# First unit's row maxima over two key chunks as fp32 products of separately projected heads

## The chip, the cores and the metric

One core of one Trainium2 chip runs the whole program, one launch. The metric is the device time in microseconds. PE is the matrix engine, PEld its weight loads, DVE is VectorE, ACT ScalarE, POOL GpSimd, SP the engine that issues most DMAs.

## The reference

Two transformer layers over x of 2048 tokens x 128. Layer 0's attention has 16 heads of 8 columns over all 2048 keys; only that stands near the change.

```python
h = _layernorm(x, axis=-1) * (1 + ca) + sa
x = x + ga * _L0_attn_ref(h, ...)
# _L0_attn_ref:
q = (x @ Wq.T + bq).reshape(b, s, NHEADS, DK)      # NHEADS 16, DK 8, s 2048
k = (x @ Wk.T + bk).reshape(b, s, NHEADS, DK)
v = (x @ Wv.T + bv).reshape(b, s, NHEADS, DV)
w = jnp.einsum('bshd,bzhd->bhsz', q, k) / jnp.sqrt(jnp.float32(DV))
w = jax.nn.softmax(w, axis=-1)
vw = jnp.einsum('bhsz,bzhd->bshd', w, v).reshape(b, s, NHEADS * DV)
out = vw @ Wo.T + bo
```

Behind it stand layer 0's mixture of experts and layer 1 (a causal attention of 8 heads and a token mix).

## The kernel before, in words

Tokens go in four chunks of 512. A unit of layer 0 is one chunk of queries and one quad of four heads (16 units, `UNITS[0]`). For each unit the softmax's row maxima are taken first: 32 score tiles (four blocks of 128 queries, four key chunks, two pairs of heads), each two products of 128 queries x 512 keys into the two halves of a double bank S0 or S1 (`s`, L918), and one VectorE maximum over each (L1283). The maxima are turned into three bf16 rows (`neg`, `neg_turn`, L938, L1515) and sent by DMA into rows of Qs (L1942), so that the transposed scores (`st`, L958) come out shifted; ScalarE takes their exponential (L1530), and PE multiplies by the values (`pv`, L990). Maxima of the next unit run beside the exponentials of this one.

q and k of a head are stored as bf16 parts in 48 rows of Qs and Ks, so that one bf16 product over 48 rows has close to fp32 accuracy. To get there a chunk is projected in fp32 (`project`, L872), brought to SBUF by ScalarE with its bias (L1483, L1486), its high part is cast (L1490), the low parts are made by three steps (`split`, on VectorE L1222 to L1226 or on GpSimd L1684 to L1688), the three parts are stored to DRAM (L1897) and loaded again with heads placed on rows (`load`, L1911 for k, L770 for q). The splits of chunks use memory in turns (`split_memory`: three own places, then two of `qf` and `q3` alternately), so ScalarE waits with the next user of a place until the store of the last one has landed (`rows_stored`).

For chunk 0 and the first quad the path over DRAM is cut short: selection matrices (`pick`, in Vf) pick the parts of the heads by bf16 products into PSUM (L881, L889), and ScalarE (L1494) and VectorE (L1230) copy them to Ks and Qs.

`make_plan` writes one order of stages by hand and by due times; every engine walks it and takes its own part, in order. A PSUM bank (T0 to T2, O, S0, S1) is handed on in the order of `take`. Beside the 32 tiles of the first unit the plan puts the other projections, `mod`, `gates`, `rows` (small products with the modulation weights) and the four `values` (v of a chunk, L897), by the number i of the tile; i counts from 0 here, so tile 31 is the first unit's last.

## Time and profile before

| | us |
|---|---|
| median of 3 runs | 1084.54 |
| lowest, highest | 1083.62, 1086.57 |
| the profiled execution | 1081.58 |
| its span in the trace | 1079.9 |
| outside the span | 1.7 |
| PE, DVE, ACT, POOL busy | 1006.4, 900.6, 823.0, 195.7 |

Busy times of PE are modelled, with the latency of each product in it, so two products that overlap count as one stretch. All stretches below are in us from the start of the span. A row of the timeline merges instructions of one line that follow each other: start, length in all, engine, line, operation, output and inputs, the count of records, and in brackets how long the engine idled ahead and for whom. An fp32 product leaves two records, a bf16 one leaves one.

### The profile page before, as it was taken

Reading aid. Unit: us, or ns where it says so; the run is one execution under the profiler, and the core shown is the slowest. Engines: PE = TensorE matmul, PEld = TensorE weight load, DVE = VectorE, ACT = ScalarE, POOL = GpSimd, SP = SyncE. Lnnn points to the kernel's source line nnn. Section 1 sums busy time; section 2 is a strip of 40 time slices with the busy share of each in tenths; the row PEclk is TensorE's granted clock in tenths of the full one; section 3 lists DMA queues with packets and bytes.
Section 4 is the critical chain, followed back from the end, with each engine's and each line's share of the span. In section 5 each row is a group of like instructions: output and inputs, shape, how many; then the busy total and the mean of one; then the engine's idle time right before and its main releaser. Section 6 shows DMA issues by size and latency. Waiting matters only on the chain.

```text
span 1079.9 us, 22190 instructions
## 1 busy us (share of the span) xinstructions
PE 1006.4 (93%) x8662; PEld 341.5 (32%) x8662; DVE 900.6 (83%) x1153; ACT 823.0 (76%) x1580; POOL 195.7 (18%) x374
## 2 busy tenths in 40 slices
PE   6879999999999999999998899999989998899997
PEld 2322222222222222222232244333344563333324
DVE  8999999999999999999989677766778868897504
ACT  4249999998999998999987577576755676656785
POOL 4542200003000003000024200241042113110102
PEclk9679999999999999999999899999999999999997
DMA  3830511000000000000000441115200531200000
GB/s 99 182 102 9 140 32 28 4 2 2 2 2 2 2 2 2 2 2 2 3 2 30 149 131 45 40 34 93 35 2 9 147 100 40 32 10 1 1 11 11
DMA packets 46423, 41.68 MB, mean 39 GB/s; under 512 B 5599, under 2 KB 44479, under 8 KB 46319
## 3 DMA queue, kind: packets, MB, share of 16 engines
q1 hardware_dynamic: 44062, 34.87, 13.3%
q0 software_dynamic: 1824, 5.25, 1.7%
q8 instruction: 70, 1.15, 0.5%
q14 instruction: 35, 0.28, 0.1%
q10 hardware_dynamic: 432, 0.13, 0.0%
HBM read 26.44 MB, written 13.30 MB: 37 GB/s over the span
## 4 chain that ended last, share of the span: by engine, by line
PE 72%; DVE 13%; ACT 8%; issue 4%; DMA 1%; POOL 1%; SPq 0%; another core or an unknown queue 0%; ACTq 0%; DVEq 0%; POOLq 0%
PE O L990 26%; PE T L958 14%; DVE mx L1283 8%; PE S L918 8%; ACT PT L1530 5%; PE S L925 4%; PE T L967 4%; PE S L1105 2%; PE S L1071 1%; ACT PT L1524 1%; PE S L1061 1%; PE T L1113 1%; PE T L999 1%; PE S L967 1%; PE T L1093 1%
## 5 line engine op out<-in xcount | busy, mean ns | idle before, releaser
L1283 DVE TENSOR_REDUCE mx<-S 128x2 f32<-128x1024 f32 (+2 forms) x672 | 759.5, 1181 | 71.7 <-PE S L918 24.4
L1530 ACT ACTIVATE PT<-T 128x512 f32<-128x512 f32 (+2 forms) x1280 | 675.7, 580 | 116.8 <-PE T L967 49.1
L990 PE MATMUL O<-PT,Va 128*9 128x256 f32 (+1 forms) x4032 | 318.1, 387 | 3.3 <-ACT Os L1564 3.3
L918 PE MATMUL S<-Ks,Qs 48*128 48x512 bf16 x1024 | 204.4, 391 | 13.3 <-DVE mx L1283 11.2
L958 PE MATMUL T<-Qs,Ks 51*128 51x512 bf16 x1024 | 202.3, 387 | 12.1 <-ACT PT L1530 7.1
L958 PEld LDWEIGHTS T<-Qs,Ks 51*128 51x128 bf16 x1024 | 56.2, 93 | 223.8 <-issue 128.6
L990 PEld LDWEIGHTS O<-PT,Va 128*9 128x9 f32 x4032 | 59.8, 88 | 208.1 <-issue 198.5
L925 PE MATMUL S<-K,Qs 96*128 96x512 bf16 (+3 forms) x320 | 89.4, 349 | 5.0 <-DVE mx L1283 3.8
L967 PE MATMUL T<-Qs,K 99*128 99x512 bf16 (+3 forms) x256 | 67.4, 344 | 12.0 <-ACT PT L1530 8.3
L990 PE MATMUL O<-PT,V 128*17 128x512 f32 (+3 forms) x616 | 72.5, 540 | 0.0
L918 PEld LDWEIGHTS S<-Ks,Qs 48*128 48x128 bf16 x1024 | 52.5, 95 | 33.9 <-DVE mx L1283 27.5
L1796 POOL CAST n<-nm 128x16 bf16<-128x16 f32 x24 | 5.5, 228 | 307.3 <-DVE nm L1291 307.1
L1696 POOL TENSOR_SCALAR_AFFINE_SELECT PT<-PT 128x256 f32<-128x256 f32 x64 | 25.8, 408 | 132.8 <-ACT PT L1530 103.8
L925 PEld LDWEIGHTS S<-K,Qs 96*128 96x128 bf16 x320 | 28.3, 97 | 48.3 <-DVE mx L1283 18.9
L1811 POOL TENSOR_TENSOR vw<-om,rl 128x128 f32<-128x128 f32 x16 | 6.5, 407 | 183.7 <-DVE rl L1297 183.7
L967 PEld LDWEIGHTS T<-Qs,K 99*128 99x128 bf16 x256 | 19.3, 98 | 49.7 <-issue 36.9
L1524 ACT ACTIVATE PT<-S 128x1024 f32<-128x1024 f32 (+3 forms) x32 | 28.4, 943 | 2.7 <-PE S L967 2.5
L928 PE MATMUL S<-mq,idb 128*128 128x128 bf16 x128 | 25.7, 220 | 0.0
L1856 POOL DMA_INDIRECT XP<-sorted_y,posu x16 | 15.8, 990 | 38.7 <-DMA sorted_y<-Vf 34.5
L1515 ACT ACTIVATE nrow<-T 12x512 bf16<-12x512 bf16 x24 | 14.1, 586 | 11.4 <-PE T L938 11.0
L1246 DVE RECIPROCAL rl<-O 128x4 f32<-128x4 f32 x3 | 0.5, 172 | 26.3 <-PE O L1026 26.3
L1607 ACT ACTIVATE Vf<-S 128x512 f32<-128x512 f32 x16 | 9.5, 595 | 15.3 <-PE S L1061 11.4
(300 smaller groups left out, 825.6 us busy)
## 6 DMA issues: line engine op xcount, KB each, us to landing
Qs<-in_L_ffn_experts SPq DMA_DIRECT2D x28, 192.0 KB, 2.5
Ks<-in_L_ffn_experts SPq DMA_DIRECT2D x20, 192.0 KB, 2.5
Vf<-sorted_x SPq DMA_DIRECT2D x12, 256.0 KB, 4.5
sorted_y<-Vf SPq DMA_DIRECT2D x12, 256.0 KB, 2.3
Qs<-rows_q SPq DMA_DIRECT2D x24, 128.0 KB, 4.5
rows_q<-q SPq DMA_DIRECT2D x7, 384.0 KB, 2.5
Qs<-rows_q SPq DMA_DIRECT2D x36, 64.0 KB
sorted_x<-XP POOLq DMA_DIRECT2D x1, 1792.0 KB, 10.7
```

Source lines behind the costliest of these rows:

```text
L918: m = e.matmul(two[:, i, :], Qs[r0:r0 + 48, hp, q0:q0 + 128], Ks[r0:r0 + 48, hp, CH * kb:CH * kb + CH], start=True, stop=True, tile_positi ...
L925: m = e.matmul(two[:, i, 0:n], Q1[0:96, 4 * quad + 2 * pair + i, q0:q0 + 128], K1[0:96, CH * kb:CH * kb + n], start=True, stop=True)
L928: m = e.matmul(two[:, i, n - 128:n], idb[:, :], mq[:, :], start=False, stop=True, skip_group_check=True)
L958: m = e.matmul(bank, Ks[r0:r0 + 51, hp, keys], Qs[r0:r0 + 51, hp, CH * c:CH * c + CH], start=True, stop=True, tile_position=(r0, 0))
L967: m = e.matmul(bank[:, lo:CH], K1[0:99, keys], Q1[0:99, 4 * quad + 2 * pair + i, CH * c + lo:CH * c + CH], start=True, stop=True)
L990: m = e.matmul(acc[32 * g:32 * g + d1, lo:hi], v, PT[(2 * j + g // 2) % 4][:, p0 + lo:p0 + hi], start=fresh, stop=True, skip_group_check=n ...
L1105: m = e.matmul(two[:, h, 128 * k:128 * k + 128], w_of(g, 2 * p + k)[:, 128 * h:128 * h + 128], hS[p % 2][:, 128 * k:128 * k + 128], start= ...
L1283: e.tensor_reduce(mx[:, u % 2, h0:h0 + 2, kb], two[:, :, 0:n], AX.X, ALU.max).then_inc(free, 1)
L1524: e.activation(both, Sb[turn["st", L, j, 2 * pair][0]][:, :, lo:CH], ACT.Exp).then_inc(free, 1)
L1530: e.activation(PT[(2 * j + pair) % 4][:, CH * i + lo:CH * i + CH], bank[:, lo:CH], ACT.Exp).then_inc(free, 1)
L1696: e.affine_select(out=both, in_=both, compare_op=ALU.is_ge, fill=0.0, base=0, pattern=[[0, 2], [1, 128]], channel_multiplier=-1).then_inc( ...
L1856: e.indirect_dma_start(out=XP[:, t, :], out_offset=None, in_=sorted_y[g], in_offset=off(posu[:, t:t + 1])).then_inc(y_gathered[c], 16)
```

## The change

The picks are gone. For the first unit's tiles against key chunks 0 and 1 (`direct`: layer 0, unit 0, kb < 2, the first 16 tiles) the four heads are projected once more, in fp32, with weights whose columns are placed so that each of the four heads has its own 8 rows at 0, 32, 64 and 96 (`place_w`, two VectorE copies; `place_bias`, two products with a placed identity). ScalarE brings the results with bias to kd and qd in Vf. A score tile is then two fp32 products over 8 rows, in two row groups, in place of two bf16 products over 48 rows.

All row splits of layer 0 are now on GpSimd. Chunk 0 of q and k also goes over DRAM now, in another order: q0, k2, k3, k1, k0 and then q1 to q3 (`raw`, `load`). q0 and k2 are loaded in two parts (2 head pairs first, 6 later), the others whole. Chunk 3's norm moves from VectorE to ScalarE, with three more small GpSimd steps. wmod is loaded behind the first loads. `mod`, `gates`, `rows` and `values` stand closer together among tiles 17 to 30, and the halves of q1 to q3 at tiles 16 to 29.

```diff
 
-PARTS = {("k", c): 2 for c in range(4)} | {("q", 0): 2}
-
-PICKED = (("k", 0), ("q", 0))
-PART_OF = {"k": (0, 1, 2, 0, 1, 0), "q": (0, 0, 0, 1, 1, 2)}
+PARTS = {("q", 0): 2, ("k", 2): 2}
 
...
+
+
+def direct(L, u, qt, kb):
+
+    return (L, u) == (0, 0) and kb < 2
 
...
@@ -297,34 +292,38 @@
             setup1(s + 3, 3)
 
 
+    def raw(kind, c, bank):
+
+        P.project(kind, c, bank)
+        P.split(kind, c, "po")
+
+    def direct_rows(kind, i, bank):
+
+        P.take(("direct", kind, i), bank)
+        P.stage("direct", kind, i)
+
+    def load(kind, c, part=0):
+        P.stage("load", kind, c, part)
+
     P.stage("silu")
     P.stage("stats", 0, 0)
     P.take(("mod", 0), "T2")
     P.stage("mod", 0)
     P.norm(0, 0)
+    P.stage("place_w")
+    P.take(("place_bias",), "S0a")
+    P.stage("place_bias")
     P.turn_h(0, 0, "T0")
-    project("k", 0, "S1b")
+    direct_rows("q", 0, "T1")
     P.stage("bias_q")
     P.stage("stats", 0, 1)
-    project("q", 0, "S1a")
+    direct_rows("k", 0, "T2")
     P.stage("stats", 0, 2)
     P.norm(0, 1)
-    P.turn_h(0, 1, "T1")
+    direct_rows("q", 1, "O")
+    P.turn_h(0, 1, "T0")
     P.stage("stats", 0, 3)
     P.norm(0, 2)
-    split("k", 0, "dv")
-    split("q", 0, "dv")
-    load_slabs()
-    for kind, pair, bank in (("k", 0, "S0a"), ("q", 0, "S0b"), ("k", 1, "S1b"), ("q", 1, "S1a")):
-        P.take(("pick", kind, pair), bank)
-    P.norm(0, 3)
-    P.stage("pick_high")
-    project("k", 1, "T2")
-    split("k", 1, "po")
-    for kind, pair in (("k", 0), ("q", 0), ("k", 1), ("q", 1)):
-        P.stage("pick", kind, pair)
-    P.turn_h(0, 2, "T0")
-    load_slabs()
 
     def values(c):
         P.take(("v", c), ("O", "T2")[c % 2])
...
@@ -474,35 +473,43 @@
 
     for i in range(many[0]):
         emit_s()
-        if i == 1:
-            project("k", 2, "O")
-            split("k", 2, "po")
-            P.stage("wmod_loads")
-            P.turn_h(0, 3, "T1")
-            load_slabs()
+        if i == 0:
+            raw("q", 0, "T1")
+        elif i == 1:
+            P.turn_h(0, 2, "T0")
+            P.norm(0, 3)
         elif i == 3:
-            project("k", 3, "T2")
-            split("k", 3, "po")
-            load_rest(("k", 0))
-            load_slabs()
-            load_rest(("k", 1))
+            raw("k", 2, "T2")
+            load("q", 0)
+        elif i == 4:
+            P.turn_h(0, 3, "T0")
+        elif i == 5:
+            direct_rows("k", 1, "T1")
+            load("k", 2)
+        elif i == 7:
             P.stage("broadcast")
-        elif i in (5, 7, 9, 11, 13, 15):
-            project_q(1 + (i - 5) // 4, (i - 5) // 2 % 2)
-            if i == 7:
-                load_rest(("q", 0))
-            elif i == 11:
-                load_rest(("k", 2), ("k", 3))
-            elif i == 15:
+            raw("k", 3, "O")
+        elif i == 10:
+            raw("k", 1, "T2")
+            load("q", 0, 1)
+            load("k", 3)
+        elif i == 13:
+            raw("k", 0, "T1")
+            load("k", 2, 1)
+            load("k", 1)
+            load("k", 0)
+        elif i in (16, 18, 23, 25, 27, 29):
+            project_q(*((1, 0), (1, 1), (2, 0), (2, 1), (3, 0), (3, 1))[(16, 18, 23, 25, 27, 29).index(i)])
+            if i == 18:
                 P.stage("constants")
-        elif i == 18:
+        elif i == 17:
             beside("mod", 1)
+        elif i == 19:
+            beside("gates")
         elif i == 20:
-            beside("gates")
-        elif i == 22:
             beside("rows")
-        elif i in (25, 27, 29, 31):
-            values((i - 25) // 2)
+        elif i in (21, 22, 26, 30):
+            values((21, 22, 26, 30).index(i))
     for i in range(7):
         if i == 2:
             urgent.pop(0)[1]()
...
-        pick = Vf[:, 0:768].bitcast(BF16).rearrange("p (k s h m) -> p k s h m", k=2, s=3, h=2)
+        kd, qd = Vf[:, 0:1024].rearrange("p (c n) -> p c n", c=2), Vf[:, 1024:1536]
+        placed_w = {"k": Vf[:, 1536:1664], "q": Vf[:, 1664:1792]}
+        idp, bd = Vf[:, 1792:1920], Vf[:, 1920:1922]
         hS, tS, acS = ([Vf[:, 6656 + 512 * k + 256 * i:6656 + 512 * k + 256 * i + 256] for i in range(2)] for k in range(3))
         Kf = Ks[:, :, :].rearrange("p a n -> p (a n)")
...
                         m.then_inc(full, 1)
-                elif name == "pick_high":
-                    pe.wait_ge(picks_made, 12)
-                    for k, kind in enumerate(("k", "q")):
-                        pe.wait_ge(high_part, P.slot[kind, 0] + 1)
-                        for pair in range(2):
-                            bank, _ = opened(("pick", kind, pair))
-                            e.matmul(bank, pick[:, k, 0, pair, :], split_memory(kind, 0)[3][:, 0, :], start=True, stop=False)
-                elif name == "pick":
-
-                    kind, pair = a
-                    bank, full = opened(("pick", kind, pair))
-                    k = int(kind == "q")
-                    pe.wait_ge(low_parts["dv"], P.split_eng[kind, 0][1])
-                    for part in (1, 2):
-                        m = e.matmul(bank, pick[:, k, part, pair, :], split_memory(kind, 0)[3][:, part, :], start=False, stop=part == 2)
-                    m.then_inc(full, 1)
+                elif name == "place_bias":
+                    bank, full = opened(("place_bias",))
+                    pe.wait_ge(ld_w0, 64)
+                    pe.wait_ge(id_placed, 1)
+                    e.matmul(bank[:, 0:1], idp, bk[:, :], start=True, stop=True)
+                    e.matmul(bank[:, 1:2], idp, bq[:, :], start=True, stop=True).then_inc(full, 1)
+                elif name == "direct":
+                    kind, i = a
+                    bank, full = opened(("direct", kind, i))
+                    c, n0, n1 = (i, 0, CH) if kind == "k" else (0, 256 * i, 256 * i + 256)
+                    done(("turn", 0, c))
+                    pe.wait_ge(w_placed, 2)
+                    e.matmul(bank[:, n0:n1], placed_w[kind], hc(c, n0, n1), start=True, stop=True).then_inc(full, 1)
                 elif name == "values":
                     (c,) = a
                     bank, full = opened(("v", c))
...
                     q0 = CH * c + 128 * qt
-                    if L == 0:
+                    if direct(L, u, qt, kb):
+                        done(("direct", "k", kb))
+                        done(("direct", "q", qt // 2))
+                        for i in range(2):
+                            r0 = 32 * (2 * pair + i)
+                            m = e.matmul(two[:, i, :], qd[r0:r0 + 8, q0:q0 + 128], kd[r0:r0 + 8, kb, :], start=True, stop=True,
+                                         tile_position=(r0, 0))
+                    elif L == 0:
                         rows_in(c, quad, pair, kb)
                         hp = 2 * quad + pair
                         for i in range(2):
...
                     m.then_inc(free, 1)
+                elif name == "place_w":
+                    dv.wait_ge(ld_w0, 64)
+                    e.tensor_copy(from_32(placed_w["k"]), by_head(wkT[:, :])).then_inc(w_placed, 1)
+                    e.tensor_copy(from_32(placed_w["q"]), by_head(wqT[:, :])).then_inc(w_placed, 1)
+                elif name == "place_bias":
+                    bank, free = filled(("place_bias",))
+                    e.tensor_copy(bd[:, 0:1], bank[:, 0:1])
+                    e.tensor_scalar(bd[:, 1:2], bank[:, 1:2], 8.0 ** -0.5, None, ALU.mult).then_inc(free, 1)
                 elif name == "bias_q":
                     dv.wait_ge(ld_w0, 64)
                     e.tensor_scalar(bqs[:, :], bq[:, :], 8.0 ** -0.5, None, ALU.mult).then_inc(bq_scaled, 1)
...
                     e.activation(parts[:, 0, :], f, ACT.Copy).then_inc(high_part, 1)
-                elif name == "pick" and a[0] == "k":
-                    kind, pair = a
-                    bank, free = filled(("pick", kind, pair))
-                    e.activation(Ks[0:112, pair, 0:CH], bank[0:112, :], ACT.Copy).then_inc(free, 1)
+                elif name == "direct":
+                    kind, i = a
+                    bank, free = filled(("direct", kind, i))
+                    done(("place_bias",))
+                    if kind == "k":
+                        e.activation(kd[:, i, :], bank, ACT.Identity, bias=bd[:, 0:1], scale=1.0).then_inc(free, 1)
+                    else:
+                        half = slice(256 * i, 256 * i + 256)
+                        e.activation(qd[:, half], bank[:, half], ACT.Identity, bias=bd[:, 1:2], scale=8.0 ** -0.5).then_inc(free, 1)
+                elif name == "norm" and a == [0, 3]:
+                    ac.wait_ge(ln_normed[0], 3)
+                    ac.wait_ge(ln_scale[0], 4)
+                    passed(P.xh_prev[0, 3])
+                    for t in range(12, 16):
+                        m = e.activation(x_hat(0, t), xs[:, t, :], ACT.Identity, bias=nb[:, t - 12:t - 11], scale=rs[:, t:t + 1])
+                    m.then_inc(ln_normed[0], 1)
                 elif name == "values":
                     (c,) = a
...
             e.dma_start(bv[:, :], col(A["L0_attn_bv"])).then_inc(ld_v, 16)
+            e.dma_start(wm_sb[0][:, 256:768], A["L0_wmod"][:, 256:768]).then_inc(ld_wm, 16)
+            e.dma_start(wm_sb[1][:, 0:768], A["L1_wmod"]).then_inc(ld_wm, 16)
             for name, *a in order:
                 if name == "split":
                     kind, c = a
```

How the order of instructions moves, at the three places of which the prediction speaks. First PE from the first projections on. L872 projects, L859 turns a chunk, L881 and L889 are the picks, L918 the score tiles. Before:

```order
L872 MATMUL S<-hT,wkT 128x512
L872 MATMUL S<-hT,wqT 128x512
L859 MATMUL T<-idf,xh 128x128 x4
L881 MATMUL S<-PT,Vf 128x512 x4
L872 MATMUL T<-hT,wkT 128x512
L889 MATMUL S<-PT,Vf 128x512 x8
L859 MATMUL T<-idf,xh 128x128 x4
L918 MATMUL S<-Ks,Qs 128x512 x4
```

The same place in the changed kernel, where L894 are the placed projections, L866 the turn, L922 the fp32 tiles and L879 a projection for the row parts:

```order
L894 MATMUL T<-hT,Vf 128x256
L894 MATMUL T<-hT,Vf 128x512
L894 MATMUL O<-hT,Vf 128x256
L866 MATMUL T<-idf,xh 128x128 x4
L922 MATMUL S<-Vf 128x512 x2
L879 MATMUL T<-hT,wqT 128x512
L922 MATMUL S<-Vf 128x512 x2
L866 MATMUL T<-idf,xh 128x128 x4
L922 MATMUL S<-Vf 128x512 x4
L879 MATMUL T<-hT,wkT 128x512
L922 MATMUL S<-Vf 128x512 x2
```

The picks between projection and tiles are gone, and whole 512-column products now stand among the tiles.

Second, SP's queue around the store of q1 (`rows_q<-q3`, the first of them), with what each waits for. Before:

```order
L1911 DMA Ks<-rows_k 8x6x512
L1897 DMA rows_q<-q3 128x3x512 [waits low_parts_po]
L770 DMA Qs<-rows_q 8x6x512 [waits rows_stored1]
L770 DMA Qs<-rows_q 8x6x512 x11
L1897 DMA rows_q<-q3 128x3x512 [waits low_parts_po]
L1911 DMA Ks<-rows_k 24x6x512
L1911 DMA Ks<-rows_k 16x6x512
```

Changed kernel, from the load of k0 on:

```order
L1952 DMA Ks<-rows_k 24x8x512 [waits rows_stored3]
L1952 DMA Ks<-rows_k 16x8x512
L1952 DMA Ks<-rows_k 8x8x512
L1952 DMA Ks<-rows_k 24x8x512
L1952 DMA Ks<-rows_k 16x8x512
L1952 DMA Ks<-rows_k 8x8x512
L1938 DMA rows_q<-q3 128x3x512 [waits low_parts_po]
L1969 DMA Ks<-K1 3x8x2048 [waits po_const]
L1969 DMA Ks<-K1 3x8x2048
L1938 DMA rows_q<-q3 128x3x512 [waits low_parts_po] x2
L1978 DMA Qs<-nrow 3x512 [waits free_T0]
```

The store of q1 stood ahead of the second parts of q0, k2 and k3; now it stands behind every load of k.

Third, PE at the end of the first unit; L897 or L901 are `values`, here of chunk 3 into T2. Before, tiles 30 and 31, `values`, and the next unit's first tile:

```order
L918 MATMUL S0<-Ks,Qs 128x512 [waits free_S0]
L918 MATMUL S0<-Ks,Qs 128x512
L918 MATMUL S1<-Ks,Qs 128x512 [waits free_S1]
L918 MATMUL S1<-Ks,Qs 128x512
L897 MATMUL T2<-wvT,hT 128x128 [waits free_T2]
L897 MATMUL T2<-wvT,hT 128x128 x3
L918 MATMUL S0<-Ks,Qs 128x512 [waits q_loaded0_1,k_loaded0_1,free_S0]
```

Changed kernel, from the second half of q3 (L879) on:

```order
L879 MATMUL T2<-hT,wqT 128x256
L929 MATMUL S0<-Ks,Qs 128x512 [waits free_S0]
L929 MATMUL S0<-Ks,Qs 128x512
L901 MATMUL T2<-wvT,hT 128x128 [waits free_T2]
L901 MATMUL T2<-wvT,hT 128x128 x3
L929 MATMUL S1<-Ks,Qs 128x512 [waits free_S1]
L929 MATMUL S1<-Ks,Qs 128x512
L929 MATMUL S0<-Ks,Qs 128x512 [waits q_loaded0_1,k_loaded0_0,free_S0]
```

and ScalarE beside it (L1503 brings a chunk of q to `qf`, L1510 casts it, L1530 copies `values` to Va):

```order
L1503 ACTIVATE qf<-T1,bqs 128x512 [waits rows_stored3,full_T1]
L1510 ACTIVATE q3<-qf 128x512 [waits free_T1]
L1530 ACTIVATE Va<-O 128x64x8 [waits full_O]
L1503 ACTIVATE qf<-T2,bqs 128x512 [waits rows_stored4,full_T2]
L1510 ACTIVATE q3<-qf 128x512 [waits free_T2]
L1530 ACTIVATE Va<-T2 128x64x8 [waits full_T2]
```

q3 now uses T2 directly ahead of `values` of chunk 3, and tile 31 stands behind both.

## Rows read from the trace of the kernel before

**Rows 1.** The page, part 2: busy tenths of VectorE in 40 slices.
```profile
DVE  8999999999999999999989677766778868897504
```
**Rows 2.** Windows of 40 us: busy (instructions) per engine, PEclk, DMA share, GB/s.
```profile
core 0: us, PE busy (x) PEld busy (x) DVE busy (x) ACT busy (x) POOL busy (x), PEclk, DMA share, GB/s
120.00:160.00 40.00, 39.42 (x420) 9.08 (x416) 39.50 (x37) 38.17 (x72) 4.14 (x32) 1.00 0.38 96
```
**Rows 3.** Timeline of VectorE's maxima: start, us, engine, line, operation, count.
```profile
20.84 4.79 DVE L1283 TENSOR_REDUCE mx<-S 128x2 f32<-128x1024 f32 x4
...
26.14 17.53 DVE L1283 TENSOR_REDUCE mx<-S 128x2 f32<-128x1024 f32 x15 [0.50 <-PE S L918]
...
59.59 1.22 DVE L1283 TENSOR_REDUCE mx<-S 128x2 f32<-128x1024 f32 x1
...
60.98 12.80 DVE L1283 TENSOR_REDUCE mx<-S 128x2 f32<-128x1024 f32 x11
```
**Rows 4.** Timeline of PE: projections, a turn and the first score tiles.
```profile
10.93 2.08 PE L872 MATMUL S<-hT,wkT 128*128 128x512 f32 x2 [0.87 <-ACT hT L1474]
...
12.80 1.92 PE L872 MATMUL S<-hT,wqT 128*128 128x512 f32 x2
...
16.92 1.10 PE L872 MATMUL T<-hT,wkT 128*128 128x512 f32 x2 [0.15 <-ACT hT L1474]
...
19.88 0.60 PE L859 MATMUL T<-idf,xh 128*128 128x128 f32 x4
...
20.41 0.81 PE L918 MATMUL S<-Ks,Qs 48*128 48x512 bf16 x4
```
**Rows 5.** Timeline of PE: score tiles, `mod`, `values`, a half of `pv`.
```profile
28.55 0.39 PE L918 MATMUL S<-Ks,Qs 48*128 48x512 bf16 x2 [0.74 <-DVE mx L1283]
...
30.82 0.61 PE L918 MATMUL S<-Ks,Qs 48*128 48x512 bf16 x2 [0.56 <-DVE mx L1283]
...
42.00 2.72 PE L832 MATMUL T<-cs,XP 128*128 128x1 f32 x12
...
56.66 1.16 PE L897 MATMUL O<-wvT,hT 128*128 128x128 f32 x8
...
79.37 0.62 PE L990 MATMUL O<-PT,Va 128*9 128x256 f32 x8
```
**Rows 6.** Timeline of ScalarE and GpSimd: cast and first split steps of a chunk.
```profile
23.23 0.63 ACT L1490 ACTIVATE q<-qf 128x512 bf16<-128x512 f32 x1
...
23.94 1.15 POOL L1684 TENSOR_TENSOR qf<-qf,q 128x512 f32<-128x512 f32 x1 [1.39 <-ACT q L1490]
...
25.16 0.61 POOL L1686 CAST q<-qf 128x512 bf16<-128x512 f32 x1
```
**Rows 7.** Timeline of SP's queue: stores (L1897) and loads (L1911) of row parts.
```profile
32.41 0.39 SPq L1897 DMA_DIRECT2D rows_k<-q  x1
32.84 7.13 SPq L1911 DMA_DIRECT2D Ks<-rows_k  x18
40.02 0.39 SPq L1897 DMA_DIRECT2D rows_q<-q  x1
...
53.61 0.38 SPq L1897 DMA_DIRECT2D rows_q<-q  x1
```
**Rows 8.** Issues of q1's and q3's store (last number: us to landing); ScalarE's wait.
```profile
rows_q<-q SPq DMA_DIRECT2D x1, 384.0 KB, 6.7
...
rows_q<-q SPq DMA_DIRECT2D x1, 384.0 KB, 7.8
...
46.79 0.69 ACT L1483 ACTIVATE qf<-T,bqs 128x512 f32<-128x512 f32 x1 [9.87 <-DMA rows_q<-q]
```
**Rows 9.** Windows of 10 us, columns as in rows 2.
```profile
30.00:40.00 10.00, 9.24 (x26) 2.83 (x24) 9.73 (x9) 2.63 (x4) 7.80 (x10) 0.50 0.85 195
40.00:50.00 10.00, 9.28 (x40) 5.99 (x38) 8.21 (x12) 1.96 (x4) 1.77 (x3) 0.50 0.87 173
50.00:60.00 10.00, 7.54 (x50) 4.64 (x48) 10.00 (x10) 2.08 (x5) 1.43 (x3) 0.99 0.74 173
```
**Rows 10.** Timeline of PE: the first transposed scores.
```profile
67.86 0.61 PE L958 MATMUL T<-Qs,Ks 51*128 51x512 bf16 x2 [0.47 <-DMA Qs<-nrow]
```

49 lines of the change are left out of this document (21 added, 28 removed).

## The prediction

> **What bounds the kernel now.** I read the page first. VectorE is at 9 tenths in the first half of the span [rows 1], and the windows of 40 us give it 39.50 us of work in 40 there [rows 2]: for the sixteen units of layer 0 its row maxima set the pace, PE merely looks as full (its ends are modelled). So what counts is when this stream of maxima starts and whether it is ever broken before it is steady. The timeline of VectorE shows both [rows 3]: the first maximum starts at 20.84, 15 of them in one piece take 17.53 (1.17 us each), the last of the first unit starts at 59.59, and the next unit's 11 follow without a gap. The whole first unit (32 maxima, 37.4 us at 1.17) takes 38.75 us from its first start to its last start, where 31 x 1.17 = 36.3 would do: 2.5 us are lost, mostly to the cold `mod` job of 2.72 us [rows 5]. Any shift of the maximum of tile 31 goes through to the end one for one, since a stretch 39.50/40 full can't take it back.
>
> **Part 1, the start.** Removed ahead of the first maximum: VectorE's six split steps and its two pick copies, twelve pick products. The two whole projections run from 10.93 to 14.72 [rows 4]; the change streams the same 1024 columns (256 + 512 + 256) through the placed weights, so it is at 14.7 too. Then stands the turn of chunk 1 (0.60 at the full clock [rows 4], up to twice that at half), so the first fp32 tile may start at 15.6. ScalarE's evictions of kd and qd (0.69 at 512 columns [rows 8]) lie beside the later products. VectorE's small new copies (some 0.5 us) lie ahead of 15.6.
>
> **Part 2, the price of an fp32 tile.** The trace has none with two row groups. Upper bound: two products one behind the other, 2 x 1.10 less an overlap of ends, 1.95. Lower bound: one product alone, 1.10 the project of 16.92 [rows 4]. I take 1.08, near the lower one, because both row groups ran side by side in bf16 (two records, 0.39 together) and four column groups of fp32 ran side by side (eight records, 0.62) [rows 5]. Where the granted clock is 0.50 (1.2 GHz) the bf16 tile takes 0.61 instead of 0.39 [rows 5, 9]. The projects at 10.93 and 12.80 took 2.08 and 1.92, that at 16.92 took 1.10 [rows 4]: by their durations the first two ran at the half clock and the last at 2.4 GHz. PE has no hole from 10.9 on in the new order either, so I take the full clock for the tiles; at half a tile would take 1.95.
>
> Now the walk through the 16 fp32 tiles. Among them stand six 512-column products (q0, k2, k3, k1, k0, direct k1) and two turns: 16 x 1.08 + 6 x 1.10 + 2 x 0.60 = 25.1. Ends overlap the next start by 0.17 within one kind (7 times; 0.21 at half clock, where the project at 12.80 starts before the end of the one at 10.93 [rows 4]) and by 0.08 at a change of kind (16 times; the tile at 20.41 starts 0.07 before the turn's end at 20.48 [rows 4]): -2.5. S0 and S1 come free 1.22 after a maximum starts [rows 3], which makes PE wait 1.1 in all. So PE ends tile 15 at 15.6 + 23.7 = 39.3; VectorE began at 16.7, was short of a tile after each job (3.5 us in sum), and starts tile 16 at 40.8. Before it starts it at 26.14 + 12 x 1.17 = 40.2. The four microseconds won at the start are gone by tile 16: part 2 is worth about +0.6 us. Tiles 16 to 31 are bf16 again at 0.39, with thirteen jobs among them; at 2.4 GHz the same walk has VectorE at tile 31 at 59.0, 0.6 before the old 59.59. That alone would be no change.
>
> Here a page speaks against the change: the Trainium skill, "TensorEngine Tiling (Array Packing)", Key Properties, says that a change of tiling mode drains the array. The row at 20.41 shows a smaller overlap, not a full drain. With a full drain the 16 changes would give up 16 x 0.08 = 1.3 us more, which would move the no-change case below by +1.3.
>
> **Part 3, the chain behind the row transfers.** This is the term that decides. The old kernel took unit 0's chunk 0 from PSUM by the picks and loaded the rest early. The new one must send q0 and k2 through memory first, and the loads of k1 and k0, whole, come last (the order of SP). The order shows a new chain: ScalarE's eviction of q3 waits for `rows_stored4`, that is for the store of q1; SP issues this store behind the loads of k2, k1 and k0; PE's `values` of chunk 3, ahead of tile 31, wants T2, which is free only when q3 is evicted; and PE is in order, so tiles 31 and up wait. So does unit 1's first tile, for k0 itself.
>
> When does it start? POOL's split takes 1.15 + 0.61 + 1.15 and ScalarE's two steps 0.69 + 0.63 [rows 6, 8]. In my walk k1's product ends at 33.0, ScalarE at 34.4, POOL at 37.4: SP stores k1 at 37.4. Up to and with the store of q1 follow 8 transfers: stores of k1, k0, q1 (3 x 384 KB), q0 for 6 heads (576), k3 (768), k2 for 6 heads (576), k1 and k0 (2 x 768) = 4608 KB. SP's own issuing (0.38 each) is done by about 53.5, also with the wait for k0's store, which comes out of 6.7 us of queue like q1's store before [rows 7, 8]. How long the bytes take: the trace moved 173 GB/s from 40 to 60 [rows 9], which gives 27.3 us; the old kernel's own queue had from the store at 32.41 to the landing of q3's store at 53.61 + 7.8 = 61.4 [rows 7, 8] exactly the same 4608 KB (4 stores, 4 k loads of 576, one of 192, q0's 576), 29 us. So landing between 64.7 and 66.4; since these stretches weren't always fed, I take 65.
>
> Then: eviction 0.69, `values` at 1.2 GHz after an idle PE (1.16 at the full clock [rows 5], so some 2.0), tile 31 0.61 [rows 5]: VectorE starts tile 31 at 65 + 0.69 + 2.0 + 0.61 = 68.3, against 59.59: **+8.7 us**. The shift rows follow by the same chain (old first transposed score at 67.86 [rows 10], new about 76.5), so nothing else becomes late. The old kernel had the same form of wait, hidden: ScalarE stood 9.87 us for q1's store until 46.79 [rows 8], with no `values` behind it.
>
> The Trainium skill, "DMA: Bandwidth & Descriptors", on how many engines a DMA uses, says that a copy with 8 rows runs on 8 of the 16 engines. By that the fullest engine carries 384 KB here against 376 KB in the old 29 us, and the landing would be at 67.0; no row here shows single engines.
>
> **Sum.** -4.1 at the start, +4.7 by the fp32 tiles and their jobs, -1.2 by the second half, then a wait of 9.3 for the transfers: +8.7. The norm of chunk 3 on ScalarE, wmod's earlier load (behind x in the queue) and POOL's extra steps cost nothing: ScalarE has little to do there (2.63 us of work from 30 to 40 [rows 9]), and POOL would be through with k0's split some 3 us before SP comes to its store. On the profiled execution 1081.58 + 8.7 = 1090.3; it lies 3.0 under the median of the three runs, so against the median: 1084.54 + 8.7 = 1093.2.
>
> **Rivals.** (A) The forecast, slower by the transfer chain: landing of q1's store between 61 and 68 moves tile 31 by 4.7 to 11.7, 1089.2 to 1096.2. It decides as soon as the store lands after 55.9, when `values` 3 could start; 4608 KB from 38.4 on would need 270 GB/s for that, and no window of ten microseconds has over 195 [rows 9]. Chance 0.60. (B) The transfers are nearly in time: whole-chunk loads make fewer, bigger transfers, and a share of 0.74 to 0.87 of the DMA engines [rows 9] leaves some room. Then the walk holds, -0.6 to +3: 1084 to 1087.5, a little less if ends overlap more. Chance 0.20. (C) PE paces: row groups don't overlap in fp32, or the eight-row products leave the clock at 1.2 GHz. With 1.95 a tile the walk ends at 72.2 instead of 59.6, and with the queue behind it +12 to +16, 1096 to 1100; with the low level all through up to +27, 1111. For it: no such row exists. Against it stands the side by side of [rows 5]. Chance 0.12. (D) Faster: the jobs slip between the tiles without stopping VectorE, transfers in time. Then up to 4.1 of the start and up to 2 of the old stalls are won, 1078.5 to 1081. Chance 0.08.
>
> **Numbers.** A measurement of this kernel can tell about 0.3%, 3.3 us. Faster: D and a bit of B, 0.09. Slower: A, C, and none of B, of A all but the lowest tenth: 0.68. Same: 0.23. The range 1083 to 1100 leaves out D, the lower edge of B (together 0.13) and the far part of C (0.07).
>
> **What would show it.** In the new trace: first maximum at about 16.7 (18 or more means PE still at 1.2 GHz); fp32 tiles of 1.1 (rows of 1.9: C); tile 16 near 41; ScalarE's last eviction of q waiting for "DMA rows_q" until about 65, a gap of 8 to 10 us in VectorE's maxima ahead of tile 31 or 32; the first transposed scores at about 76; the windows from 120 on unchanged. I am wrong if that gap is missing or ends before 60, or if layer 0 takes the shift back.

## The result, and the profile after

The changed kernel takes 1111.25 us (median of 4 runs, 1106.61 to 1112.79) beside 1085.55 us for the kernel before on the same chip (4 runs, 1083.62 to 1086.61): a ratio of 1.0237, 95% interval 1.0218 to 1.0256, **25.7 us slower**. The forecast was 1093.2 us with a range of 1083 to 1100. Its sign was right, its size was not, and the range did not hold the time. The span of the profiled execution is 1109.4 us.

VectorE's row maxima again show the whole story (timeline of VectorE after; columns: start, us, engine, line, operation, tiles, count, then in brackets the idle time before it and who ended it). To be held against [rows 3].

```profile
16.73 1.23 DVE L1303 TENSOR_REDUCE mx<-S 128x2 f32<-128x1024 f32 x1 [1.42 <-PE S L922]
...
33.33 2.36 DVE L1303 TENSOR_REDUCE mx<-S 128x2 f32<-128x1024 f32 x2 [2.79 <-PE S L922]
...
52.19 4.85 DVE L1303 TENSOR_REDUCE mx<-S 128x2 f32<-128x1024 f32 x4 [2.79 <-PE S L922]
...
68.67 9.15 DVE L1303 TENSOR_REDUCE mx<-S 128x2 f32<-128x1024 f32 x8 [0.18 <-PE S L929]
84.97 1.23 DVE L1303 TENSOR_REDUCE mx<-S 128x2 f32<-128x1024 f32 x1 [7.15 <-PE S L929]
```

The first maximum starts at 16.73 (16.7 forecast). The group at 52.19 is tiles 14 to 17, so tile 16 starts at 54.6 where 40.8 was forecast. Tile 31 starts at 84.97, behind a wait of 7.15. In the kernel before it was 59.59 [rows 3], so tile 31 is 25.4 us late: -4.1 at the start, +18.5 over the first sixteen tiles (37.9 us from the first maximum to tile 16 instead of 19.4), +3.9 over tiles 16 to 30, +7.15 by the wait. These four come to 25.4, and the whole kernel is 25.7 us longer.

Where the 18.5 us come from stands in the windows (us of the window, busy us and instructions of each engine, PEclk, DMA share, GB/s), which answer to [rows 9]:

```profile
core 0: us, PE busy (x) PEld busy (x) DVE busy (x) ACT busy (x) POOL busy (x), PEclk, DMA share, GB/s
15.00:20.00 5.00, 5.00 (x19) 2.07 (x19) 2.69 (x4) 2.72 (x5) 1.99 (x4) 0.90 0.00 2
20.00:25.00 5.00, 5.00 (x12) 1.56 (x12) 2.43 (x3) 2.70 (x7) 2.13 (x3) 0.50 0.23 79
25.00:30.00 5.00, 5.00 (x13) 1.72 (x10) 1.91 (x2) 1.38 (x2) 4.18 (x6) 0.50 0.06 22
...
60.00:65.00 5.00, 5.00 (x20) 3.21 (x20) 2.75 (x4) 2.37 (x5) 3.15 (x4) 0.50 0.89 174
65.00:70.00 5.00, 4.62 (x26) 3.20 (x26) 3.71 (x4) 1.20 (x2) 0.00 (x0) 0.82 0.88 128
```

TensorE is busy 5.00 us of 5 from 15 to 30, and still its granted clock falls from 1.00 (2.4 GHz) to 0.50 (1.2 GHz) just before 20 us (0.90 in that window) and stays there to about 67 (0.82 in the last window). The rows of TensorE (timeline; 8*128 8x512 are the operands' shapes) show what that does:

```profile
15.54 1.14 PE L922 MATMUL S<-Vf 8*128 8x512 f32 x4
16.61 1.12 PE L879 MATMUL T<-hT,wqT 128*128 128x512 f32 x2
17.67 1.13 PE L922 MATMUL S<-Vf 8*128 8x512 f32 x4
...
22.13 2.08 PE L879 MATMUL T<-hT,wkT 128*128 128x512 f32 x2
24.14 2.08 PE L922 MATMUL S<-Vf 8*128 8x512 f32 x4
```

At the full clock an fp32 tile takes 1.14 (1.08 forecast): its two row groups do run side by side. At half it takes 2.08 (1.95 forecast), and so do the projections among the tiles. VectorE needs 1.2 us a tile and stands idle for the rest.

The transfers (timeline of SP's queue, which answers to [rows 7]; L1938 stores, L1952 loads) and then ScalarE's timeline with its wait, as in [rows 8]:

```profile
47.27 0.38 SPq L1938 DMA_DIRECT2D rows_k<-q  x1
...
55.11 14.78 SPq L1952 DMA_DIRECT2D Ks<-rows_k  x18
69.93 0.67 SPq L1938 DMA_DIRECT2D rows_q<-q  x1
70.64 3.76 SPq L1969 DMA_DIRECT2D Ks<-K  x2
```

```profile
81.57 0.69 ACT L1503 ACTIVATE qf<-T,bqs 128x512 f32<-128x512 f32 x1 [8.37 <-DMA rows_q<-q]
```

q1's store is issued behind 18 loads of 2112 KB in all, which take 14.78 us to issue (before: 18 of 1344 KB in 7.13 [rows 7]), and lands at 81.5. ScalarE waits 8.37 us for it with q3's eviction, and the wait of 7.15 ahead of tile 31 follows. That is the forecast's chain, every link of it.

### The profile page after: what moved, and what is told of

Read it like the earlier page. It is cut to its first block, busy times and chain, and to the rows that moved or that the text cites. A ratio compares the mean times of both kernels' runs of the same rounds, so it can differ in the third digit from the quotient of the medians.

```text
span 1109.4 us, 22247 instructions
## 1 busy us (share of the span) xinstructions
PE 1029.5 (93%) x8694; PEld 351.1 (32%) x8694; DVE 895.2 (81%) x1134; ACT 827.9 (75%) x1586; POOL 202.6 (18%) x382
## 3 DMA queue, kind: packets, MB, share of 16 engines
q1 hardware_dynamic: 44398, 35.27, 13.2%
## 4 chain that ended last, share of the span: by engine, by line
PE 70%; DVE 10%; ACT 8%; DMA 4%; issue 4%; SPq 2%; POOL 1%; another core or an unknown queue 1%; ACTq 0%; DVEq 0%; POOLq 0%
PE O L1001 25%; PE T L969 14%; PE S L929 8%; DVE mx L1303 6%; ACT PT L1562 4%; PE S L936 4%; PE T L978 3%; PE S L1116 2%; PE S L922 2%; DMA rows_q<-q 1%; PE S L1082 1%; ACT PT L1556 1%; PE T L879 1%; PE S L1072 1%; PE T L1124 1%
## 5 line engine op out<-in xcount | busy, mean ns | idle before, releaser
L929 PE MATMUL S<-Ks,Qs 48*128 48x512 bf16 x992 | 197.2, 388 | 10.4 <-DVE mx L1303 8.1
L929 PEld LDWEIGHTS S<-Ks,Qs 48*128 48x128 bf16 x992 | 50.8, 95 | 29.0 <-DVE mx L1303 21.9
L922 PE MATMUL S<-Vf 8*128 8x512 f32 x64 | 22.1, 1075 | 2.1 <-DVE mx L1303 2.1
L1362 DVE SCALAR_TENSOR_TENSOR Vf<-Vf,S 128x512 f32<-128x512 f32 x16 | 10.9, 682 | 14.9 <-ACT Vf L1639 14.0
```

Of the source, the lines that this page charges most:

```text
L922: m = e.matmul(two[:, i, :], qd[r0:r0 + 8, q0:q0 + 128], kd[r0:r0 + 8, kb, :], start=True, stop=True, tile_position=(r0, 0))
L929: m = e.matmul(two[:, i, :], Qs[r0:r0 + 48, hp, q0:q0 + 128], Ks[r0:r0 + 48, hp, CH * kb:CH * kb + CH], start=True, stop=True, tile_positi ...
```

## The experiments

The kernel before ran on the same chip each time; the last column is the difference of the medians to it, and the intervals are those of the ratio, at 95%. "First st" is the first transposed score (67.86 before [rows 10]), which sums up what the first unit lost: in the timed kernels it shifts by 4 to 25 us, and the time follows it within 3.4 us. All edits are shown shortened. e4, e7 and e16 add up the scores of several heads in the first 16 tiles, so they show times and not a usable kernel.

| kernel | tile 16 starts | wait ahead of tile 31 or 32 | first st | us against before |
|---|---|---|---|---|
| before | 40.2 | none | 67.86 | 0 |
| after | 54.6 | 7.15 | 93.06 | +25.7 |
| after again (e15) | 52.6 | 8.96 | 90.92 | +23.75 |
| q3 moved (e10) | 57.4 | none | 91.57 | +21.2 |
| q3's own place (e3) | 52.5 | 3.25 | 87.18 | +19.0 |
| 32 rows (e1) | 43.6 | 8.36 | 83.17 | +13.75 |
| 64 rows (e7) | 41.1 | 9.75 | 82.88 | +14.3 |
| 64 rows, k0 first, q3 moved (e16) | 42.6 | none | 78.96 | +7.9 |
| bf16 (e2) | 35.4 | 9.33 | 76.76 | +7.85 |
| bf16, q3's own place (e5) | 36.7 | 4.90 | 74.22 | +5.0 |
| the same, k0 first (e6) | 34.9 | 1.48 | 72.11 | +3.3 |

**The clock, and the width of the products.** Four kernels change the tiles alone (columns of the windows below as above). In e1, e7 and e4 the products go over more rows of the array:

```
-  qd[r0:r0 + 8, q0:q0 + 128], kd[r0:r0 + 8, kb, :]      tile_position=(r0, 0), r0 = 32 * (2 * pair + i)
+  qd[r0:r0 + 32, ...], kd[r0:r0 + 32, ...]              e1: the further 24 rows are zero
+  qd[r0:r0 + 64, ...], kd[r0:r0 + 64, ...]              e7: r0 = 64 * i, two heads added up
+  qd[:, ...], kd[:, ...]                                e4: no tile_position, all heads added up
```

> The changed kernel with one edit: the fp32 tiles take all 32 rows of each row group instead of the 8 of the head; the 24 others hold zeros, so the result is the same. Theory 1: PE's clock falls at 20 us because the fp32 tiles use only 16 of 128 rows at a time, so that the chip counts PE as little used. If rows by instruction count (not by value), the granted clock stays at 1.00 from 20 to 50, the tile stays at 1.14, tile 16 starts near 41 instead of 54.6, and the time falls by 7 to 14 us to about 1097 to 1104 (the store of q1 then still holds tile 31 up, near 68 to 75). Rival 2: the clock falls for another reason (the waits between tiles, or just the time since the start): windows 20 to 50 at 0.50, tiles 2.08, 1111 as the changed kernel. Rival 3: it is the values that count (zeros are no work): as rival 2.

> The changed kernel with each fp32 tile's two products over 64 rows each (rows 0 to 63 beside rows 64 to 127, still two row groups side by side), so that all 128 rows take part; a product then adds up two heads, so the scores of those 16 tiles are not the reference's, their size and order are. Theory 1 (the clock falls because few rows of the array take part; with the pair still side by side): granted clock 1.00 through 20 to 55 us, tile 1.14, tile 16 at 41 to 43, tile 31 behind the wait for q1's store at 68 to 72, time before + 8 to + 12 us: what is left is the transfer chain alone. Rival (the fall comes from two fp32 products running side by side, and the 128-row version that kept the clock did so because its products ran one behind the other): clock down to 0.50 from about 20 as in the changed kernel, tiles 2.08, before + 24 to + 27.

> The changed kernel, but each of the two fp32 products of the first 16 tiles runs over all 128 rows, one behind the other, without row groups. Leaves out the separation of heads in these 16 tiles (the scores of four heads are summed), so their maxima are others. Shows the clock and the price of a tile without row groups: theory 1 has the granted clock at 1.00 throughout 20 to 50, as all rows are in use; a tile takes 1.95 to 2.1 (twice 1.10 less overlap) at the full clock, tile 16 starts near 52. If the clock still falls to 0.50, a tile takes 3.9 and the time is near 1135 to 1140, and theory 1 is out.

Measured: e1 1090.7 us (+13.75, ratio 1.0131, 1.0103 to 1.0158), e7 1092.19 (+14.3, 1.0141, 1.0111 to 1.0170), e4 one run, 1098.83 (+21.9). The windows of e1, e7 and e4, in this order, and of e16 (the table's other kernel with 64 rows):

```profile
25.00:30.00 5.00, 5.00 (x20) 1.50 (x18) 4.01 (x4) 2.00 (x3) 3.53 (x6) 1.00 0.33 98
30.00:35.00 5.00, 4.80 (x16) 1.19 (x14) 2.79 (x3) 1.32 (x2) 2.53 (x4) 0.67 0.23 59
...
45.00:50.00 5.00, 5.00 (x20) 3.46 (x20) 3.03 (x7) 0.84 (x2) 0.00 (x0) 0.50 0.97 156
```

```profile
25.00:30.00 5.00, 5.00 (x20) 1.67 (x18) 3.49 (x4) 2.00 (x3) 3.01 (x6) 1.00 0.34 99
...
45.00:50.00 5.00, 5.00 (x34) 3.31 (x32) 4.93 (x5) 2.58 (x6) 3.15 (x4) 1.00 0.98 163
```

```profile
30.00:35.00 5.00, 5.00 (x13) 2.28 (x12) 2.63 (x3) 1.36 (x3) 1.33 (x3) 1.00 0.39 117
...
45.00:50.00 5.00, 5.00 (x14) 2.04 (x13) 2.90 (x3) 1.32 (x2) 2.31 (x3) 1.00 0.61 145
```

```profile
40.00:45.00 5.00, 4.42 (x27) 2.33 (x23) 4.75 (x6) 0.53 (x1) 2.91 (x3) 0.96 0.67 152
45.00:50.00 5.00, 5.00 (x18) 3.25 (x18) 3.37 (x6) 1.91 (x3) 2.31 (x3) 0.50 0.99 147
```

With 8 rows a group the clock falls just before 20 us (in e15 at 22 to 23). With 32 it holds past 31 us, comes back for three us before 40 and is then low to 55. With 64 beside 64 it holds through all sixteen fp32 tiles: to 50 in e7, to about 44.6 in e16. With 128 it holds past 50. From 15 to 30 us, where the first kernels part, they have the same columns, the same place in the program and a TensorE that is busy 5.00 of 5. So the busy time does not tell them apart, and the rows that the products take part in do. e7 also answers the rival that the pair side by side in fp32 is the cause: the pair is kept there, every one of its tiles takes 1.13, and the clock stays. e1's further rows hold only zeros, so what they gain does not come from their values. Each width has one trace, 64 rows two and 8 rows four, and why rows should count is not shown. e4 also shows what a tile costs without the pair: 1.88 us.

VectorE's timeline of e7:

```profile
38.77 4.62 DVE L1303 TENSOR_REDUCE mx<-S 128x2 f32<-128x1024 f32 x4 [0.89 <-PE S L922]
...
55.19 3.49 DVE L1303 TENSOR_REDUCE mx<-S 128x2 f32<-128x1024 f32 x3 [4.45 <-PE S L929]
...
74.80 1.23 DVE L1303 TENSOR_REDUCE mx<-S 128x2 f32<-128x1024 f32 x1 [9.75 <-PE S L929]
```

The first group is tiles 14 to 17: with the clock up, tile 16 starts at 41.1 against the 40.8 of the forecast. From the first maximum (16.16) that is 24.9 us, where the changed kernel took 37.9 and the kernel before 19.4. So 13.0 of the 18.5 us are the clock's, and 5.5 (4.7 forecast) are the price of the fp32 tiles and their jobs at the full clock. In the time of the whole kernel the clock is worth less, 9.5 us against e15 and 11.4 against the first measurement, since earlier tiles then wait longer for the transfers (4.45 and 9.75 above).

Of the expectations, e1's time came (7 to 14 us less than the changed kernel), its clock of 1.00 to 50 us did not. e7's clock to 50, its tiles and tile 16 came; its tile 31 (68 to 72) and its time (+8 to +12) did not. e4's clock came, its tile 16 starts at 50.7 (52).

e2 puts the direct rows into bf16 (a tile is 0.39 then):

```
-  kd, qd = Vf[:, 0:1024]..., Vf[:, 1024:1536]
+  kd, qd = Vf[:, 0:512].bitcast(BF16)..., Vf[:, 1024:1280].bitcast(BF16)
```

> The changed kernel with kd and qd as bf16 instead of fp32, so that a tile is two bf16 products over 8 rows in two row groups (one pass, 512 columns). The maxima are then less exact, which the softmax only sees as another shift. Takes away the fp32 price alone. If the fp32 tiles at half clock (2.08) are what paces the first 16 tiles, each tile now takes 0.39 or 0.61 and what is left are the six whole projections (2.08 at half clock): tile 16 near 40 to 43 instead of 54.6, tile 31 then held by the store of q1 until 68 to 75; time 1095 to 1103. If other things pace them (ScalarE, the order of jobs), the time stays within 4 us of 1111. The clock: theory 1 (few rows) has it at 0.50 here as well.

Measured: 1084.8 us, +7.85 (1.0067, 1.0046 to 1.0087). Tile 16 starts at 35.4 (40 to 43 expected), five us ahead of the kernel before, and the clock, expected at 0.50 here too, holds to about 29 us. The five us are lost again, as VectorE's timeline of e2 shows:

```profile
50.20 9.14 DVE L1303 TENSOR_REDUCE mx<-S 128x2 f32<-128x1024 f32 x8 [0.70 <-PE S L929]
68.68 1.23 DVE L1303 TENSOR_REDUCE mx<-S 128x2 f32<-128x1024 f32 x1 [9.33 <-PE S L929]
```

The transfer chain alone puts tile 31 at 68.68, though these tiles hardly hold VectorE up.

**The chain.** e3 gives q3's rows a place (and a semaphore) of their own, so that their eviction waits for no store. e10 leaves the places and moves q3's two half projections from beside tiles 27 and 29 to behind tiles 35 and 37.

```
 def split_memory(kind, c):
+    if n == 7:
+        return 5, 0, Vf[0:rows, 2048:2560], Vf[0:rows, 2560:3328]...        e3
...
-        elif i in (16, 18, 23, 25, 27, 29):
+        elif i in (16, 18, 23, 25):                                          e10
...
+        if i in (3, 5):
+            project_q(3, i // 4)
```

> The changed kernel with one wait taken away by memory: chunk 3 of q gets its own place for fp32 and bf16 parts, so ScalarE's eviction of q3 no longer waits for the store of q1 (8.37 us in the trace of the changed kernel, ahead of a 7.15 us gap in VectorE's maxima before tile 31). Theory A (this chain costs the gap): the gap shrinks to 0 to 2 us and the time falls by 5 to 7.5, to 1104 to 1106. Rival: the load of k0, which the next unit's first tile wants, lands no earlier than the store of q1 did, so the gap moves behind tile 31: the time falls by under 3 us, and the new gap is ahead of tile 32 and waits for DMA Ks<-rows_k.

> The changed kernel with one move alone: q3's projections, its eviction and its three low parts come after tiles 35 and 37, behind the row of negative maxima, instead of beside tiles 27 and 29. Products, types and places are the changed kernel's. Theory (the gap of 7.15 us ahead of tile 31 is q3's eviction waiting for q1's store and nothing else, and the start of the transposed scores carries it to the end): no such gap, tile 31 at 77 to 78 in a trace like the changed kernel's, first transposed scores at 85 to 88 instead of 93, and 18 to 20 us above the kernel before instead of 25.7. Rival (the stores and loads as a whole are late, so the gap only moves to tile 32 or to the transposed scores): a gap of the same length there, 24 to 26 above before.

> The changed kernel itself once more, beside the others. Theory (8 rows in fp32 bring the granted clock down as soon as these tiles fill TensorE): 24 to 28 us above the kernel before; tiles 2.08 us from between 15 and 21 us to 55 at least, tile 31 at 84 to 87, first transposed scores at 92 to 95. Rival (the fall at 20 us was the luck of one execution): the low stretch begins 5 us later or more, or ends earlier, and the time is under before + 20.

Measured: e3 1095.93 us, +19.0 (1.0185, 1.0145 to 1.0224); e10 1098.32, +21.2 (1.0186, 1.0167 to 1.0204); the changed kernel itself once more (e15) 1101.47, +23.75 (1.0232, 1.0205 to 1.0259), its clock falling at 22 to 23 us, three later than in the first trace; the time is just under the 24 to 28 expected. In both repairs the long wait ahead of tile 31 is gone (VectorE of e10, where these nine are tiles 23 to 31):

```profile
72.42 10.27 DVE L1305 TENSOR_REDUCE mx<-S 128x2 f32<-128x1024 f32 x9 [0.89 <-PE S L931]
```

So q3's eviction behind q1's store is what held tile 31. But beside e15 e3 wins 4.8 us and e10 2.5, less than e15's wait of 8.96 (and the intervals of e3 and e15 overlap): in e3 tile 32 then has a wait of 3.25 us, for k0's rows by what e6 below shows (the trace names no releaser), so theory and rival both came in part. e10 missed its 18 to 20. And e10's execution ran its tiles at the low clock from the first on:

```profile
15.51 2.08 PE L924 MATMUL S<-Vf 8*128 8x512 f32 x4
17.52 2.08 PE L881 MATMUL T<-hT,wqT 128*128 128x512 f32 x2
```

```profile
20.00:25.00 5.00, 5.00 (x17) 1.66 (x15) 1.52 (x2) 3.26 (x7) 2.92 (x3) 1.00 0.00 0
```

The second fence is the window of that same trace: it says 1.00 beside products that take 2.08. The row is wrong there; durations decide. The Trainium skill, "TensorE: Matmul & The Clock Gate", Part 1, warns that the recorded clock events can be unreliable, and this trace agrees: 2.08 us under a 1.00.

This bears on the comparison of 8-row kernels. The longest executions of the changed kernel (1112.79), of e15 (1102.95, 1105.40), e3 (1102.25) and e10 (1099.03, 1099.25) have a recorded mean clock of 0.979 to 0.985, the shorter ones 0.956 to 0.968. By e10's trace the higher record can mean a low stretch that was not recorded; for the others no trace shows it. Among executions with the lower record e15 takes 1098.27 and 1099.99, e10 1096.48 and 1097.61, e3 1094.19 to 1096.96.

**Both, and the order of the loads.** e5 is e2 with e3's place. e6 also projects k0 ahead of k1 and loads k0, k1, then k2's rest. e8 moves q1's projections to beside tiles 14 and 15. e16 is the fp32 kernel over 64 rows with k0 first and q3 moved.

```
-            raw("k", 0, "T1"); load("k", 2, 1); load("k", 1); load("k", 0)
+            raw("k", 1, "T1"); load("k", 0); load("k", 1); load("k", 2, 1)      e6
-        elif i in (16, 18, 23, 25, 27, 29):
+        elif i in (14, 15, 23, 25, 27, 29):                                      e8
```

> The changed kernel with both edits: direct rows and tiles in bf16 (tile 0.39 instead of fp32), and q3's rows in a place of their own, so that their eviction waits for no store. Theory (the two costs, the low clock and the wait for q1's store, add up, and each edit takes its own away): no wait of 9.33 ahead of tile 31, tile 31 at about 59.5, and then a wait of 1 to 4 ahead of tile 32 for k0's load, whose issue ends at 55.2; time before - 2 to + 3 us. Rival (the stores and loads on the one queue are late as a whole, so taking one wait away only uncovers the next): tile 32 at 66 or later, before + 4 to + 7.

> As the bf16 kernel with q3's own place, and k0 projected, stored and loaded ahead of k1 and of the second part of k2 (tile 32 reads k0 first). Theory (k0's load, the last of 18 issues that take 13.4 us, is what tile 32 then waits for): the wait ahead of tile 32 goes, and the time is 1 to 4 us under that of the kernel with k1 first; before - 5 to 0. Rival (tile 32 waits for nothing of the transfers, or for all of them alike): the same time as with k1 first, within 1 us.

> As the kernel with k0 first, and q1's projections moved from beside tiles 16 and 18 to beside tiles 14 and 15, where TensorE has room, so that q1's rows are ready earlier. Theory (after the other two repairs TensorE's jobs of the second stretch, 1.3 us waits ahead of tiles 18 to 22, are what costs): two of these waits go, tile 31 0.7 to 1.5 us earlier, before - 6 to - 1. Rival (tile 32 and the transposed scores are bound by the transfers, so tiles that come earlier only wait there): the time of the kernel with k0 first, within 1 us.

> The changed kernel in fp32 with three edits: products over 64 rows each (all 128 rows take part; the scores of those 16 tiles then add up two heads), k0 projected, stored and loaded ahead of k1, and q3's work behind the row of negative maxima. Theory (low clock and transfer chain are the whole loss): clock at 1.00 to 50 us, no wait over 2 us ahead of tile 31 or 32, tile 31 at 63 to 66, first transposed scores at 74 to 76, before + 4 to + 7. Rival (the third wait, 4.45 us ahead of tile 24 for k3's rows, stays, since the walk arrives before them): tile 31 at 67 to 69, before + 8 to + 11.

Measured: e5 1082.89 us, +5.0 (1.0043, 1.0027 to 1.0059); e6 1081.2, +3.3 (1.0034, 1.0021 to 1.0046); e8 1081.07, +3.2 (1.0027, 1.0014 to 1.0039); e16 1085.59, +7.9 (1.0070, 1.0048 to 1.0093). The theory for e5 was half right: the wait of 9.33 becomes one of 4.90 at tile 32. The time is in the rival's range (+4 to +7), above the -2 to +3 of the theory. k0 first takes that wait away, and the median falls by 1.7 us; the two intervals overlap. e8 is the rival's: no change. e16 is the fp32 kernel with the clock up to about 44.6 us, through all fp32 tiles, and without a wait ahead of tile 31 or 32: still 7.9 us slower (+4 to +7 expected, the clock to 50). TensorE's first transposed score in e16 names what it waits for:

```profile
78.96 0.61 PE L971 MATMUL T<-Qs,Ks 51*128 51x512 bf16 x2 [5.60 <-DMA Qs<-nrow]
```

**What is left.** In e6 tile 31 starts at 61.87, but the first transposed scores come at 72.1. They wait for the row of negative maxima, four transfers of 3 KB. Five kernels look for the reason: e9 (bf16, k0 first, q3 moved), e11 (e9 with q1 early), e12 (e9 with 32 rows), e13 (e11 with these four transfers issued by ScalarE), e14 (the kernel before with that edit alone).

> The bf16 kernel with k0 projected and loaded first, and with q3's work moved behind the row of negative maxima as above, in place of a rows' place of its own. Theory (with the waits for q1's store and for k0's load gone, the row of negative maxima is what the first transposed scores wait for; with q3's store no longer ahead of it on the queue it lands 3 to 4 us after its issue as in the kernel before, against 6.3 now): first transposed scores at 67 to 69, and 3 to 4 us less than the kernel with k0 first (+3.3), so before - 1 to + 1. Rival (the row is late for the four loads of maxima rows being slow behind the loads of k1 and k2 as a whole): first transposed scores at 71 to 72, + 2 to + 4.

> As the last, with q1's projections beside tiles 14 and 15 instead of 16 and 18. Theory (TensorE's jobs in the second stretch hold VectorE up by some 5 us there, in waits of 0.2 to 1.6; two jobs fewer take away 0.7 to 1.5 of it): 0.5 to 1.5 us less than the last. Rival (they only move the wait to tiles 15 to 17, since the granted clock is at 0.50 there too): the same time within 0.7 us.

> As the kernel with q3 late, and its bf16 tiles over 32 rows of each group (the 24 further ones are zero). Theory of the clock (the share of rows at work counts): the granted clock stays at 1.00 beyond 30 us and is up through part of 30 to 45, where it is 0.50 with 8 rows; jobs there take half the time, and tiles 16 to 22 come 1 to 3 us earlier; 1 to 2 us less than the kernel with q3 late. Rival (there the clock falls because TensorE has little to do, 3.2 to 3.7 us busy of 5, whatever the rows): clock and time as with 8 rows, within 0.7 us.

> The bf16 kernel with k0 first, q3 late and q1 early (+ 3.3), and the first unit's four transfers of the row of negative maxima issued by ScalarE on its own queue instead of by SyncE. Theory (they are slow because SyncE's queue still holds the row loads: four issues take 5.5 us there, against 2.8 in the kernel before): they land 3 to 4 us after the issue, first transposed scores at 67 to 69 instead of 72.2, and 2 to 4 us less: before - 1 to + 1. Rival (it is the 16 transfer engines that are full, whichever queue asks): landing after 7 us or more as on the other queue, the same time within 0.7 us.

> The kernel before with that same edit alone, as its control: the first unit's four transfers of the row of negative maxima issued by ScalarE. Theory (in the kernel before the queue is empty by then: issued at 63.4 to 66.1, landed at 67.4): first transposed scores 0 to 1.5 us earlier, before - 1.5 to 0. Rival (the four issues each take 0.65 us of ScalarE or the queue's first use costs more than SyncE's): 0 to + 2.

Measured: e9 1083.3 us, +6.2; e11 1080.42, +3.3; e12 1080.08, +3.0; e13 1082.65, +4.9 (1.0033 to 1.0061); e14 1080.81, +3.1 (1.0009 to 1.0039). e9's theory fell: q3's store isn't what the row queues behind, first transposed scores still come at 73.05. In e11 tile 31 starts at 59.50, as early as before (59.59), and the kernel is still slower: here the row alone is late. e11 is 2.9 us below e9, more than the 0.5 to 1.5 of its theory. e9 and e12 have the same trace to 0.3 us, clock included (0.72 from 25 to 30, 0.50 from 30 to 50 in both): in these two the clock fell between 25 and 30 us, in windows in which TensorE did 3.5 to 3.9 us of work in 5 (25 to 40), and the width changed nothing. The 3.2 us between their distances to the kernel before stay without a cause. e13 and e14 were not the clean test that they were meant to be: SP, freed of the row, issued its loads of the late weights ahead of it (from 56.2 in e14 instead of 66.16), and the row landed later (first transposed scores at 75.51 in e13 and 73.21 in e14). Their times lie outside both theory and rival, and they say nothing on which queue is better.

e17 is e11 with one stage moved: the two copies of the rows of ones (96 KB each, to three partitions each) are issued beside tile 5 instead of behind all row loads. e18 moves the same stage in the kernel before, from beside tile 15 to beside tile 7.

```
             direct_rows("k", 1, "T1")
+            P.stage("constants")
...
-            if i == 15:
-                P.stage("constants")
```

> The bf16 kernel with k0 first, q3 late and q1 early (+ 3.3), and one stage moved: the two copies of the rows of ones onto the rows under k (96 KB each, to three partitions each) are issued beside tile 5, at about 25 to 28 us, instead of beside tile 15, behind all row loads. Theory (these copies, which few transfer engines carry, are what the row of negative maxima queues behind): the row lands 3 to 5 us after its first issue instead of 8.4, first transposed scores at 67 to 69, before - 2 to + 0.5. Rival (it is the row loads and q2's store that it queues behind, and the transfer engines that these use are the same few): first transposed scores at 71 to 73, the time within 1 us of + 3.3; the earlier copies may hold up q0's and k2's loads besides.

> The kernel before with the same stage moved alone, from beside tile 15 to beside tile 7. Theory: there the copies are issued at 54.5 and through by the time of the row of negative maxima (its transfers wait 0.5 us only), so next to nothing changes: - 1 to + 0.5. Rival (issued at about 33 us they stand among the row loads that the tiles wait for): + 1 to + 3.

Measured: e17 1092.92 us, +9.1 (1.0084, 1.0064 to 1.0104); e18 1083.47, -0.4 (0.9999, 0.9986 to 1.0013). SP's queue and then TensorE's first transposed score, in e11 and then in e17:

```profile
55.77 2.72 SPq L1971 DMA_DIRECT2D Ks<-K  x2
58.53 0.66 SPq L1940 DMA_DIRECT2D rows_q<-q  x1
63.47 5.47 SPq L1980 DMA_DIRECT2D Qs<-nrow  x4
```

```profile
72.18 0.61 PE L971 MATMUL T<-Qs,Ks 51*128 51x512 bf16 x2 [4.06 <-DMA Qs<-nrow]
```

```profile
29.96 1.68 SPq L1970 DMA_DIRECT2D Ks<-K  x2
31.68 8.00 SPq L1953 DMA_DIRECT2D Ks<-rows_k  x6
...
72.69 2.84 SPq L1979 DMA_DIRECT2D Qs<-nrow  x4
```

```profile
77.12 0.64 PE L970 MATMUL T<-Qs,Ks 51*128 51x512 bf16 x2
```

The row is used 4.4 us after its first issue instead of 8.7: the copies of ones are most of what it queued behind. (The rival, row loads and stores still on the queue, explains little of it: from the end of the last row load's issue, 55.31 and 63.94, the row is issued after 8.2 us in e11 and 8.8 in e17, and used after 16.9 and 13.2.) But the copies cost as much where they stand now: k2's six loads behind them take 8.00 us to issue instead of 2.14. Tile 16 then has a wait of 4.28 us, for which the trace names no releaser but which fits these loads, and everything is later, so the theory's 67 to 69 and its time did not come. While they run the transfer engines are busy to 0.15 in the mean (30 to 35 us, 25 GB/s): two or three of 16 on average. The Trainium skill, "DMA: Bandwidth & Descriptors", in the part on how many engines a DMA uses, gives a copy whose outer dimension is 3 three engines, the lowest ones, and the same three to every such copy; the share of 0.15 to 0.22 and the order of the two kernels agree with it, though no row shows single engines. In the kernel before the copies are through in time either way (e18, as its theory said).

No version beats the kernel before: the best are 3.0 to 3.3 us above it, little, but with intervals above 1 (e12 1.0010 to 1.0031, e11 1.0015 to 1.0038).

## Why the prediction was wrong, point by point

**Start.** Right: first maximum at 16.73 (16.7). The small copies and the turn of chunk 1 cost what was said.

**Price of an fp32 tile.** Right at the full clock: 1.14 against 1.08, a pair side by side, near the lower bound. The modelled ends overlap by 0.07 at a change of kind, as was said. The starts show more (TensorE in e7, then in e4, whose tiles have no row groups):

```profile
18.74 1.99 PE L922 MATMUL S<-Vf 64*128 64x512 f32 x8
20.66 1.13 PE L879 MATMUL T<-hT,wkT 128*128 128x512 f32 x2
21.72 1.13 PE L922 MATMUL S<-Vf 64*128 64x512 f32 x4
```

```profile
24.02 1.02 PE L879 MATMUL T<-hT,wkT 128*128 128x512 f32 x2
24.88 1.88 PE L922 MATMUL S<-Vf 128*128 128x512 f32 x4
```

In e7 the second of the two tiles starts 0.86 after the first (1.99 - 1.13), but from the projection to the next tile it is 1.06; in e4 that same step takes 0.86. So a change between row groups and a full product costs 0.20 us, some 3 us over the forecast's 16 changes. The forecast had nearly the same spacing at a change, 1.02 (1.10 less 0.08), without calling it a price. The Trainium skill, "TensorEngine Tiling (Array Packing)", Key Properties, says that such a change drains the array; these rows agree in that it costs 0.20 us; that the array drains meanwhile no row shows.

**The step that failed** is the sentence "PE has no hole from 10.9 on in the new order either, so I take the full clock for the tiles". TensorE had no hole up to 35 us, and the clock fell all the same, before 20. The forecast took the clock to be low only behind idle time. Its own rows spoke against that: in the kernel before TensorE is busy 9.24 and 9.28 us of 10 from 30 to 50 at a granted clock of 0.50 [rows 9]. e7 shows the term by itself: with the clock up tile 16 starts at 41.1 for a forecast 40.8, with it down at 54.6. By terms: the start -4.1 (-4.1 said), tiles 0 to 15 +18.5 (+4.7), tiles 16 to 30 +3.9 (-1.2), the wait +7.15 (+9.3). The two middle terms, the first at the low clock throughout but for its start and the second up to 67 us, were set 18.9 us too low and the wait 2.2 too high, 16.7 in all; the time is 18 above the forecast, one of them because the kernel before is taken at 1085.55 here and not at 1084.54.

Rival C had named it ("the eight-row products leave the clock at 1.2 GHz", 1111 at the low level all through), but with C's whole chance at 0.12 and only 0.05 of it inside the range. It was believed too little. That its 1111 is the measured time is in part luck: it had the low level all through, and here the clock came back at 67 us and the wait of 7.15 stands in the time. The Trainium skill, "TensorE: Matmul & The Clock Gate", Part 1, ties the clock to how busy TensorE is; by that the clock would have stayed, and this trace disagrees: 0.50 beside 5.00 of 5 busy.

**The transfer chain.** The mechanism was right in every link: q1's store behind the loads, ScalarE's wait (8.37; 8 to 10 forecast), `values` 3, tile 31. Its wait in the changed kernel, 7.15 us, is near the 9.3 that was said. But e7, which has the forecast's own premise of a full clock, has k1's store at 37.64 (37.4 forecast) and tile 31 at 74.80 instead of 68.3: the 4608 KB took 33.7 us to the landing, 140 GB/s, and not 27.6 us. The mis-sized term is the rate. The 173 GB/s were read from 40 to 60 us of the old trace, and the same bytes had taken 29 us there. In e7 the 18 loads with the whole chunks take 15.39 us to issue (13.42 to 15.83 in all variants), 137 KB per us, where the old trace's 18 took 7.13, 188 KB per us. Why these loads move fewer bytes per us is not shown. e2's 68.68 hits the forecast's 68.3 only by luck: its k1 store came five us earlier, at 32.63. With the clock up through the fp32 tiles the time is +14.3 (e7), where +8.7 was said; that alone would still have been inside the range.

**What the forecast did not have**: k3's load as a wait (4.45 us ahead of tile 24 in e7), and the copies of ones in front of the row of negative maxima. It had the shift rows follow "by the same chain"; with the chain taken out they became late by themselves (e11, e16).

**The steady state.** Right: the shift at tile 31 (25.4) went through to the end (25.7). It is not the only way to lose time, though: e11's tile 31 is not late at all, and its row of negative maxima is.

## What to carry to other kernels

Before a job is put into TensorE's first microseconds as many products over few rows, look at what it does to the clock of everything that runs beside them: here 8-row fp32 products doubled the price of the projections as well. Zero rows in the same instruction cost nothing (1.13 a tile for 1.14) and kept the clock longer (+13.75 instead of +23.75 to +25.7). And a queue's rate is to be taken from transfers of the shape that will run, with the tiny ones at its end counted: here 3 KB waited four us behind two copies.

## What the runs showed of the hardware

- The granted clock can fall while TensorE is without a hole: 0.50 at 5.00 of 5 busy with 8-row fp32 products in pairs, from just before 20 us. With 32 rows a group it first fell past 31 us; with 64 beside 64 at 50 (e7) and 44.6 (e16), behind the fp32 tiles; with 128 past 50. What sets it in general is open: only these four widths were run, in one kernel, and in bf16 8 and 32 rows gave the same clock (e9, e12).
- A window's clock of 1.00 can be wrong: 2.08 us products under it from 15.5 us on (e10).
- Two fp32 row groups overlap nearly whole: 1.14 for the pair, 1.88 one behind the other over 128 rows. Each change between row groups and a full product costs 0.20 us between starts (e7 against e4).
- Two copies of 96 KB to three partitions hold back what is issued behind them: a 3 KB transfer was used after 8.7 us instead of 4.4 (e11, e17), and six loads took 8.00 us to issue instead of 2.14 (e17).
